# A five-stage transformer tower: two sums of the middle stage moved to TensorE, rounding to ScalarE, GpSimd's large operations reordered

## The reference, cut to what matters

```python
h = _layernorm(h + _L0_ffn_ref(h, ...))                # item's h2, from the stored h1 and two expert outputs

def quantum_circuit(v):
    return jnp.cumprod(jnp.cos(v), axis=-1)            # in groups of 16

attn_out = quantum_circuit(x.reshape(B, T, H, dk)).reshape(B, T, C)
x1 = layer_norm(x + attn_out, gamma1, beta1)           # x is h2
q = quantum_circuit(x1[..., :nq])                      # nq = 16
h = jnp.einsum('btq,fq->btf', q, w1) + b1              # 1024 hidden
ffn_out = jnp.einsum('btf,cf->btc', relu(h), w2) + b2
out = layer_norm(x1 + ffn_out, gamma2, beta2)
h = _layernorm(h2 + out)                               # item's h3
logits = h @ wg; top1 = argmax(...); rank = running count of earlier tokens with that expert
```

## Time and profile before

| | us |
|---|---|
| median of three runs | 1659.44 (1659.33 to 1661.4) |
| the profiled execution, its own time | 1659.89 |
| its span | 1658.2 |
| the middle, first to last instruction, about | 923.3 to 1318.5 |

### The profile page before, as it was taken

How to read it: one execution, slowest core, us unless ns; L and a number is a source line. 1 busy time by engine, 2 the same in 40 slices (tenths; PEclk the granted TensorE clock), 3 DMA queues, 4 the chain that set the end, 5 groups by cost and what they waited for, 6 DMA issues and landing times. The chain is left out here.

```text
span 1658.2 us, 23461 instructions
## 1 busy us (share of the span) xinstructions
PE 1313.6 (79%) x6824; PEld 912.0 (55%) x6824; DVE 962.8 (58%) x2728; ACT 504.5 (30%) x966; POOL 745.5 (45%) x936
## 2 busy tenths in 40 slices
PE   1267878877899839999999267777777489999997
PEld 0245555545666426666666155555555357776665
DVE  7565775776666544444444468888886424444443
ACT  1024444434555412222222234344433111111111
POOL 2552353535121234455444456656564335444553
PEclk9968788889989669999999677777777689999999
DMA  6447346444857241211121532221100181110000
GB/s 155 79 77 114 71 91 134 87 65 102 150 132 138 69 167 57 65 64 63 65 64 40 161 117 93 81 82 57 58 7 13 32 312 30 33 31 28 28 25 11
DMA packets 97449, 134.69 MB, mean 81 GB/s; under 512 B 18208, under 2 KB 80302, under 8 KB 96304
## 3 DMA queue, kind: packets, MB, share of 16 engines
q1 hardware_dynamic: 77536, 93.52, 24.3%
q0 software_dynamic: 16416, 38.46, 7.4%
q10 hardware_dynamic: 3376, 1.22, 0.4%
HBM read 75.43 MB, written 35.73 MB: 67 GB/s over the span
## 5 line engine op out<-in xcount | busy, mean ns | idle before, releaser
L966 DVE TENSOR_REDUCE top_a_a<-s_bank 128x4 f32<-128x1024 f32 x128 | 156.5, 1223 | 110.7 <-PE s_bank L616 107.3
L1506 PE MATMUL mbank<-w2T_m,fhT_m 128*128 128x256 f32 x512 | 154.6, 468 | 0.0
L792 ACT ACTIVATE prob_a<-s_bank 128x1024 f32<-128x1024 f32 x128 | 130.4, 1019 | 77.1 <-PE s_bank L637 75.4
L1935 PE MATMUL ebank<-w,exT 128*128 x312 | 142.5, 600 | 0.7 <-ACT exT L1981 0.7
L1946 PE MATMUL ebank<-w,ehT 128*128 x624 | 141.2, 379 | 0.9 <-ACT ehT L1989 0.9
L1506 PEld LDWEIGHTS mbank<-w2T_m,fhT_m 128*128 128x128 f32 x512 | 120.0, 241 | 37.3 <-ACT fhT_m L1620 10.2
L1163 PE MATMUL ebank<-w,exT 128*128 x284 | 135.5, 600 | 0.6 <-ACT exT L1210 0.6
L1175 PE MATMUL ebank<-w,ehT 128*128 x568 | 134.4, 380 | 0.8 <-ACT ehT L1216 0.8
L1122 POOL DMA_INDIRECT ex<-rows_d,tile_row x71 | 72.8, 1026 | 120.2 <-DVE sent_to L1248 102.2
L1946 PEld LDWEIGHTS ebank<-w,ehT 128*128 128x128 f32 x624 | 115.6, 190 | 15.7 <-issue 1.6
L527 POOL DMA_INDIRECT rows_d<-h_a,row_i_a x64 | 63.7, 995 | 129.9 <-DVE row_i_a L1052 115.0
(11 more groups left out here) (342 smaller groups left out, 2669.9 us busy)
## 6 DMA issues: line engine op xcount, KB each, us to landing
w<-in_L_ffn_W SPq DMA_DIRECT2D x16, 1024.0 KB, 10.0
qs_a<-parts_q_a SPq DMA_DIRECT2D x96, 128.0 KB, 4.4
ks_a<-parts_k_a SPq DMA_DIRECT2D x96, 128.0 KB, 6.4
w<-in_L_ffn_w SPq DMA_DIRECT2D x16, 512.0 KB, 5.2
image_a<-in_x SPq DMA_DIRECT2D x4, 1024.0 KB, 7.6
h_d<-rec_a SPq DMA_DIRECT2D x4, 1024.0 KB, 3.8
x_a<-h_d SPq DMA_DIRECT2D x16, 256.0 KB, 3.2
h_d<-h_a SPq DMA_DIRECT2D x16, 256.0 KB, 2.5
```

The source lines that it names most:

```text
L792: nc.scalar.activation(prob[:, j % 4].rearrange("p g t s -> p (g t s)"), s2_bank[:].rearrange("p g s -> p (g s)"), ACT.Exp, scale=HD ** -0 ...
L966: nc.vector.tensor_reduce(top[:, j].rearrange("p g t -> p (g t)"), s1_bank[:].rearrange("p g (t s) -> p (g t) s", t=TPI), axis=AX, op=ALU. ...
L1506: last = nc.tensor.matmul(b[:, t * D:(t + 1) * D], hT[:, f, t * P:(t + 1) * P], w2T[:, f, :], start=False, stop=f == FC - 1)
L1935: last = nc.tensor.matmul(bank[1 + n % 2][:], xT[j % 2][:, ch, :], w[:, bass.ds(e, 1), at:at + 512].rearrange("p a f -> p (a f)"), start=c ...
```

## The change

It has four parts.

- **h2 + running products.** L1698 goes. A new TensorE step `S2` puts the sum into bank 3 by four products with the identity; `V2` (VectorE) takes the variances from the bank, and `x1` reads the bank. `S2` and `V2` stand in the list behind `SC`.
- **x1g + F2.** R2's add goes. F2 adds x1g by a product with the identity in each half, and its row `shift1` is given as two fp32r parts in a product with 33 rows. R2's variances and B2 read the bank.
- **Turns.** ScalarE makes the turns right behind h2 by two operations on 512 columns. VectorE's RTa is one operation (C1 times the turns, off h2), and GpSimd's r1 goes. D and R lose one and one or two small copies.
- **Places.** A0 goes from the head of the list to the place ahead of root3; x1g to the place behind qc, which on GpSimd's own queue leaves it between root1 and root2. In `attention` the six fills of `ks` go from VectorE to GpSimd, behind its other constants and ahead of L445.

```diff
+            for u in range(RING):
+                for half in (32, 96):
+                    c.link(nc.gpsimd.memset(ks[u][half:half + 32].bitcast(F32), 1.0))
+            pool.sem_inc(q["ks_ok"], 2 * RING)
             pool.wait_ge(q["w_in"], 16 * 4)
...
             weigh_rest(0, last=False)
-            for u in range(RING):
-                for half in (32, 96):
-                    nc.vector.memset(ks[u][half:half + 32].bitcast(F32), 1.0).then_inc(q["ks_ok"], 1)
...
-        STEPS = [("load", "n2"), ("A0", "n1"), ("A1", "n"), ("root0", "n"), ("h2", "n"), ("SC", "m"), ("root1", "m"), ("RTa", "n"), ("r1", "n"), ("x1", "m"),
-                 ("T", "p"), ("XQ", "m"), ("x1g", "m"), ("qsin", "m"), ("D", "p"), ("rk", "p"), ("RTb", "n"), ("sin", "n"), ("prep", "n"),
-                 ("SQa", "m"), ("qc", "m"), ("R2", "f"), ("root2", "f"), ("SQb", "m"), ("F1", "m"), ("R", "p"), ("scatter", "p"),
-                 ("B2", "f"), ("root3", "f"), ("h2b", "n"), ("F2", "m"), ("h3", "f")]
+        STEPS = [("load", "n2"), ("A1", "n"), ("root0", "n"), ("h2", "n"), ("SC", "m"), ("S2", "m"), ("V2", "m"), ("root1", "m"), ("RTa", "n"), ("x1", "m"),
+                 ("T", "p"), ("XQ", "m"), ("qsin", "m"), ("D", "p"), ("rk", "p"), ("RTb", "n"), ("sin", "n"), ("prep", "n"),
+                 ("SQa", "m"), ("qc", "m"), ("x1g", "m"), ("R2", "f"), ("root2", "f"), ("SQb", "m"), ("F1", "m"), ("R", "p"), ("scatter", "p"),
+                 ("B2", "f"), ("A0", "n1"), ("root3", "f"), ("h2b", "n"), ("F2", "m"), ("h3", "f")]
...
+            def S2(i):
+                if i == 0:
+                    pe.wait_ge(q["tr_ok"], 6)
+                pe.wait_ge(q["run_ok"], i + 1)
+                if i >= 1:
+                    pe.wait_ge(q["x1_ok"], i)
+                for t in range(TPI):
+                    nc.tensor.matmul(bank[3][:, t * D:(t + 1) * D], ident[:], h2[i % 2][:, t, :], start=True, stop=False)
+                    last = nc.tensor.matmul(bank[3][:, t * D:(t + 1) * D], ident[:], run_[:, t * D:(t + 1) * D], start=False, stop=True)
+                last.then_inc(q["sum2_ok"], 1)
...
-                    nc.tensor.matmul(b[:, t * D:(t + 1) * D], ones_f[0:1, :], shift1[0:1, :], start=True, stop=False)
+                    nc.tensor.matmul(b[:, t * D:(t + 1) * D], ones_r[0:33, :], shift_hl[0:33, :], start=True, stop=False)
+                    if t == 0:
+                        pe.wait_ge(q["x1g_ok"], i + 1)
+                    nc.tensor.matmul(b[:, t * D:(t + 1) * D], ident[:], x1g[i % 2][:, t, :], start=False, stop=False)
...
+                nc.scalar.activation(turns_[:], flat(h2[i % 2]), ACT.Identity, bias=magic[:, 0:1], scale=INV).then_inc(q["t_ok"], 1)
+                act.wait_ge(q["t_ok"], i + 1)
+                nc.scalar.activation(turns_[:], turns_[:], ACT.Identity, bias=off_magic[:, 0:1]).then_inc(q["n_ok"], 1)
...
             def RTa(i):
-                dve.wait_ge(q["h2_ok"], i + 1)
-                c.link(nc.vector.tensor_scalar(turns_[:], flat(h2[i % 2]), INV, MAGIC, ALU.mult, ALU.add))
-                nc.vector.tensor_scalar(turns_[:], turns_[:], -MAGIC, -C1, ALU.add, ALU.mult).then_inc(q["n_ok"], 1)
+                dve.wait_ge(q["n_ok"], i + 1)
+                nc.vector.scalar_tensor_tensor(out=r1_[:], in0=turns_[:], scalar=-C1, in1=flat(h2[i % 2]), op0=ALU.mult, op1=ALU.add)\
+                    .then_inc(q["r1_ok"], 1)
...
                 nc.vector.tensor_tensor_scan(run_[:], cs[:], first[:], 0.0, ALU.mult, ALU.add).then_inc(q["run_ok"], 1)
-                dve.wait_ge(q["run_ok"], i + 1)
-                nc.vector.tensor_tensor(flat(sum2), run_[:], flat(h2[i % 2]), ALU.add).then_inc(q["sum2_ok"], 1)
+
+            def V2(i):
                 dve.wait_ge(q["sum2_ok"], i + 1)
-                variances(1, sum2)
+                variances(1, bank[3][:].rearrange("p (t d) -> p t d", t=TPI))
...
                 dve.wait_ge(q["f2_ps"], i + 1)
-                dve.wait_ge(q["x1g_ok"], i + 1)
-                if i >= 1:
-                    dve.wait_ge(q["z2_ok"], i)
-                nc.vector.tensor_tensor(flat(r2), bank[4 + i % 2][:], flat(x1g[i % 2]), ALU.add).then_inc(q["r2_ok"], 1)
-                dve.wait_ge(q["r2_ok"], i + 1)
-                variances(2, r2)
+                variances(2, bank[4 + i % 2][:].rearrange("p (t d) -> p t d", t=TPI))
```

More of the change, by code:

```diff
@@ L1301, in middle @@
         hT = sb("fhT", [P, FC, SEQ])
-        sum_, sum2, r2, z2, r3 = (sb(n, [P, TPI, D]) for n in ("sum_", "sum2", "r2", "z2", "r3"))
+        sum_, z2, r3 = (sb(n, [P, TPI, D]) for n in ("sum_", "z2", "r3"))
         h2 = [sb(f"h2_{u}", [P, TPI, D]) for u in range(2)]
@@ L1312, in middle @@
         shift1 = sb("shift1", [P, D])
-        ones_f = sb("ones_fm", [P, P])
+        shift_hl = sb("shift_hl", [64, D], F32R)
+        shift_hi = sb("shift_hi", [64, D], F32R)
+        ones_r = sb("ones_rm", [64, P], F32R)
         wg = sb("wg1", [P, 2, E])
-        half_pi = sb("half_pi", [P, 1])
+        half_pi, magic, off_magic = (sb(n, [P, 1]) for n in ("half_pi", "magic", "off_magic"))
         h2b = [sb(f"h2b_{u}", [P, TPI, D]) for u in range(RING)]
@@ L1454, in _ @@
                    "root1": lambda i: root(i, 1), "root2": lambda i: root(i, 2), "root3": lambda i: root(i, 3),
-                   "r1": r1, "x1g": x1g_, "h2b": h2b_, "scatter": scatter})
+                   "x1g": x1g_, "h2b": h2b_, "scatter": scatter})
             c.reset()
@@ L1568, in x1_ @@
                     act.wait_ge(q["x1g_ok"], i)
-                normal(i, 1, sum2, x1, q["x1_ok"])
+                normal(i, 1, bank[3][:].rearrange("p (t d) -> p t d", t=TPI), x1, q["x1_ok"])
             def h3_(i):
@@ L1637, in _ @@
             c.run(nc.vector.memset(half_pi[:], float(np.pi / 2)))
-            c.run(nc.vector.memset(ones_f[:], 1.0))
+            c.run(nc.vector.memset(magic[:], MAGIC))
+            c.run(nc.vector.memset(off_magic[:], -MAGIC))
+            c.run(nc.vector.memset(ones_r[:].bitcast(F32), 1.0))
+            c.run(nc.vector.memset(shift_hl[:].bitcast(F32), 0.0))
             for t in (cs, first, qcs, qfirst):
@@ L1652, in prep @@
                     nc.vector.tensor_tensor(wstack[:, :, BROW + 1], b1n[:], wstack[:, :, BROW].bitcast(F32), ALU.subtract).then_inc(q["w_ok"], 1)
-                    nc.vector.tensor_tensor(shift1[:], be1[:], b2[:], ALU.add).then_inc(q["w_ok"], 1)
+                    c.link(nc.vector.tensor_tensor(shift1[:], be1[:], b2[:], ALU.add))
+                    c.run(nc.vector.tensor_copy(shift_hl[0:1, :], shift1[0:1, :]))
+                    c.link(nc.vector.tensor_copy(shift_hi[32:33, :], shift1[32:33, :]))
+                    nc.vector.tensor_tensor(shift_hl[32:33, :], shift1[32:33, :], shift_hi[32:33, :].bitcast(F32), ALU.subtract).then_inc(q["w_ok"], 1)
             def variances(k, x):
@@ L1783, in R @@
                 nc.vector.tensor_tensor(cnt[:], bank[7][:, TPI * E:(TPI + 1) * E], cnt[:], ALU.add).then_inc(q["rk_ok"], 1)
-                c.link(nc.vector.tensor_tensor(prod[:], pick[:], rk[:], ALU.mult))
-                c.link(nc.vector.tensor_reduce(rank_f[:], prod[:], axis=AX, op=ALU.add))
-                nc.vector.scalar_tensor_tensor(out=row_i[i % 2][:], in0=idx_f[:], scalar=float(SLOTS), in1=rank_f[:],
+                c.link(nc.vector.tensor_tensor(prod[:], both[:], rk[:], ALU.mult))
+                ranks = rank1[:, TPI * i:TPI * i + TPI]
+                c.link(nc.vector.tensor_reduce(ranks, prod[:], axis=AX, op=ALU.add))
+                nc.vector.scalar_tensor_tensor(out=row_i[i % 2][:, :, 0], in0=idx_f[:, :, 0], scalar=float(SLOTS), in1=ranks,
                                                op0=ALU.mult, op1=ALU.add).then_inc(q["row_ok"], 1)
-                c.link(nc.vector.tensor_copy(rank1[:, TPI * i:TPI * i + TPI], rank_f[:, :, 0]))
                 dve.wait_ge(q["rk_ok"], i + 1)
                 dve.wait_ge(q["row_ok"], i + 1)
-            turns({"A1": A1, "SC": SC, "RTa": RTa, "RTb": RTb, "XQ": XQ, "SQa": SQa, "SQb": SQb, "R2": R2, "B2": B2, "D": D_, "R": R, "prep": prep})
+            turns({"A1": A1, "SC": SC, "V2": V2, "RTa": RTa, "RTb": RTb, "XQ": XQ, "SQa": SQa, "SQb": SQb, "R2": R2, "B2": B2, "D": D_, "R": R, "prep": prep})
             c.reset()
```

36 lines of the change are left out of this document (17 added, 19 removed).

## The result

The changed kernel takes 1746.35 us (median of 4 runs, 1740.9 to 1748.4) beside 1660.42 us for the kernel before: a ratio of 1.0505, with a 95% interval of 1.0478 to 1.0532. The forecast was 1752. The profiled execution has a span of 1744.3 us, 86.1 more than before.

What follows compares the result with a forecast made beforehand. Bound: a ring through TensorE and VectorE, tied to VectorE's queue. Fourteen turns at +6.2 (+86.8), first turn +9.5, middle's start +3.4, end -1 and kernel start -6.1 gave +92.6 on 1659.4: 1752 us, range 1707 to 1786.

Steps and rivals of the forecast that it cites:

- The ring through TensorE, T, D, RTb and SQb: Middle turns: SQb releases the next F1 and F2; 6.49 us from F2's end to SQb's end in a 21.73 us turn.
- both were tied: Middle: VectorE's queue and the ring have no slack; D begins when T's logits are there and XQ is over.
- From F2's end to D: Middle turn: S2, V2 with root1, x1 and XQ now follow F2, 8.65 us against 2.22 before.
- F1 with F2: TensorE's products in each middle turn: kept at 15.2 us, bounds 13.3 and 16.8.
- granted clock lower than now: Sign for TensorE in the middle: the gap ahead of F1 grows from 6.5 to 12.7 us.
- The first turn: Middle's first turn, not held by F2 before, would be held by it: SQb of item 1 at 988.8, +9.5 us.
- The middle's start: S2 of item 0 waits for the last copy of w2T, so V2 begins near 953: +3.4 us.
- The tail: End of the middle: one add and one small copy leave the last chain, -1 us.
- The start of the kernel: Six memsets leave VectorE's chain for GpSimd; logits start at 33.1 and not 39.23: -6.1 us, bounds -7.1 and 0.
- The other side: Rival: VectorE's queue is the real bound and S2 not in the way; 1650 us (0.04) or 1598 (0.02).
- The clock rival: TensorE's clock stays up in F2, 1717 us (up in most turns 0.07), or stays low through S2, 1830 (0.04).
- the third rival: GpSimd's memsets cancel the start's gain, 1758 us; or root1, XQ and V2 run without collisions, 1732; no separate chance given.

Runs made afterwards that it cites:

- the best kernel: Changed kernel with S2 undone, T between F2's halves, scan ahead of A1, x1 ahead of T, x1g after RTb, A0 inside scatter: 1600.8 us, ratio 0.9664.
- The last run: The best kernel with VectorE's SQb and R ahead of R2 and root2's wait behind z2: 1644.75 us, ratio 0.9887 to the kernel before.

## Why the prediction was right

**The bound.** The ring through TensorE, T, D, RTb and SQb was named as the bound beside a VectorE that is busy for 83% of the time, and S2's place behind F2 as what lengthens it. The runs with S2 undone, S2 alone, S2 twice and S2 between the halves show it one by one. But the statement that both were tied held in a stricter sense than I used: with S2 undone and F2 cut, VectorE's own queue still gave 21.4 us where nothing else came in its way.

**The turn.** From F2's end to D 8.65 us were forecast, 8.49 are there (1113.69 to 1122.18). Term by term: S2 and the step to its reader 1.90, measured 1.76; V2 and root1 2.93, measured 3.08, in which root1's first operation took 0.58 us beside RTa; x1 1.12, measured 1.05; XQ 2.70, measured 2.60. The bank cost no surcharge (0.76 against 0.75 for two statistics), as taken; the 0.3 of its upper bound came from no row. D to SQb's end is 4.03 against 4.27 in the earlier trace rows, which is the 0.2 forecast. The mis-sized term is F1 with F2: 15.2 kept, 14.8 found (27.3 - 8.5 - 4.0). So a turn is 27.3 and not 27.9 us, +5.6 and not +6.2, and over fourteen turns +78.0 (from SQb of item 1 to that of item 15, 382.3 against 304.3 us) and not +86.8. That difference of 9 us is the largest of the sum, and it is inside the range. Two errors stand against each other in it. The products ahead of the w2 products were taken to cost as much as before and cost 0.6 us more: 1.53 and 0.85 us (from 1102.73 to 1104.26 and from 1109.22 to 1110.07) against 1.14 and 0.63 (from 1114.04 to 1115.18 and from 1120.84 to 1121.47 in the kernel before). The w2 products were kept at 5.73 and 3.72 us and take 5.04 and 3.62, 0.8 less.

**The clock.** The forecast that TensorE's granted clock falls in every turn holds: within F1 it is at the lower level, 1.2 GHz, after the idle time ahead of F1. TensorE alone (us, PE busy, PEclk, DMA, GB/s):

```profile
1100.20:1101.20 1.00, 1.00 (x4) 0.50 0.00 0
```

The sign "granted clock lower than now" fails: over the turns its mean is 0.75 against 0.73 in the earlier trace rows. F2's first half takes 5.04 us in the turn shown against 5.73 in the earlier trace rows, so the clock came back a little earlier. Most of what the w2 products gained lies there; why the clock came back earlier no run settles.

**The ends.** The first turn was forecast +9.5 and is 26.8 against 18.0 us, +8.8. The middle's start was forecast +3.4 and is +3.4 between the two traces. The agreement is partly luck: this way takes 35.8 to 41.2 us in the ten traces with the sum on VectorE and 40.0 to 43.6 in the four with it on TensorE. The tail was forecast -1 and is -0.5.

**The start of the kernel.** The fills on GpSimd do what was said, and the first transfer of x begins at 51.77 against 58.45, -6.7. The logits:

```profile
32.93 0.39 PE L549 MATMUL bank<-tok_part_a,blocks_a 128*128 128x10 f32 x2 [0.69 <-ACT wT_o_a L749]
```

Forecast was 33.1. The two traces show only 3.6 us of it left at the middle's start, and I first read that as given back in the stages between. The runs say otherwise: the twelve kernels with the fills on GpSimd and the same code up to there begin the middle at 912.5 to 920.7 us, 917.1 in the mean, so a difference of 3 us between two single executions says nothing. The two with the fills on VectorE begin it at 923.3 and 921.0. The fills alone are worth 2.7 to 6.5 us by the 95% interval, 3.8 by the medians, and the forecast of 6.1 lies inside near its upper end.

**The total.** 1746.35 against 1752 is closer than the largest term was: by the two traces the turns gave 9 us less than forecast, the first turn 0.7 less, and the start took off 2.5 us less, which offsets a part of it.

**The signs.** S2 within 0.1 us of F2's end, V2 with no way around TensorE, VectorE under 60%, logits at 33: all as said. V2's wait was to be 4 to 6 us and is 7.17 in the turn shown, never under 7.1 in the turns around it, since VectorE has that much less to do ahead of it. Turns near 28 are 27.3.

**The rivals.** The other side, 1650 us if S2 were not in the way, did not come; the run with S2 undone, which leaves the other parts of the change, gave 1644.8. The clock rival (1717 or 1830) did not come either: the second half of F2 takes 3.62 us, and the first still about 5. Of the third rival, the fills alone (ratio 0.9973) show that GpSimd's memsets don't eat up the gain, and the collisions in root1 and XQ stayed (0.58 us at 1116.79, 1.14 us at 1119.80).

## What to carry to other kernels

Before work is moved to a less busy engine, look at where it stands in that engine's order: here four products that take 1.7 us together cost 27.3 - 21.5 = 5.8 us a turn behind F2, and 23.9 - 21.5 = 2.4 us between its halves. A cover that the step had in its old place (F2, under which VectorE made the sum) is part of its price. When two rings are of one length, an edit that opens only one of them measures as nothing; it is worth keeping and trying again with the other one opened. And before a step is moved ahead of another, look at what it waits for: R ahead of R2 lent its wait to R2.

## What the runs showed of the hardware

VectorE's small operations beside GpSimd's additions of 512 columns took 1.24 and 1.19 us instead of 0.19, and r3, read from SBUF, took 1.89 instead of 0.88 where A0 ran beside it. z2, which reads a bank, was not held up (0.88 beside A0). In this kernel a large operation of GpSimd cost VectorE up to 1.1 us or nothing, by what it stood beside. The Trainium skill, "SBUF — State Buffer", section "SBUF: two separate sides", counts an operation of VectorE with two inputs in SBUF among those that exclude a GpSimd operation reading SBUF; the stretched ones and r3 have two such inputs, z2 one beside the bank, and the traces agree. An operation with one input in SBUF and two columns was held up as well, in the changed kernel beside A0 (0.17 us where nothing is beside it):

```profile
1102.79 1.28 POOL L1415 TENSOR_TENSOR hin_m<-hin_m,ya_m 128x512 f32<-128x512 f32 x1
1102.80 1.31 DVE L1692 TENSOR_SCALAR minus_m_m<-moments_m_m 128x2 f32<-128x2 f32 x1
```

So two inputs in SBUF aren't the only case in which these traces show a collision.

The stages between the kernel's start and the middle vary by some 8 us between executions of kernels with the same code there. A step of 3 us can't be read from two traces; it takes rounds.

TensorE's granted clock over the turns was 0.72 to 0.75 in the kernel before, the changed one, and those with S2 undone or between the halves. In the best kernel it was 0.86:

```profile
1007.74:1216.54 208.80, 166.31 (x715) 130.83 (x715) 152.83 (x585) 111.49 (x242) 128.06 (x187) 0.86 0.22 71
```

TensorE is busy there for 80% of the time, against 73% in the earlier trace rows, and with nearly the same products it needs 15.1 us a turn (166.31 / 11) instead of 16.0 (192.36 / 12). In these traces a shorter ring went with a faster TensorE, which is a second gain on top of the first. The last run shows the same the other way: TensorE was idle for 3.6 us ahead of T and for 1.5 us behind it, the clock in the logits was 0.50, and T with the second half took 10.4 us in the mean and not 9.2.
